# The seam between the second graph attention and the three mean layers of a graph network: loads issued in the attention's tail, weights folded on GpSimd, rows joined tile by tile

## The reference, cut to what matters

```
q, k, v = x @ Wq + bq, x @ Wk + bk, x @ Wv + bv
logits = sum(q[dst] * k[src], -1) / sqrt(256)
attn = segment_softmax(logits, dst)
agg = segment_sum(attn[:, None] * v[src], dst)
h = relu(agg + x @ Ws + bs)
deg = maximum(segment_sum(1, dst), 1)
prev, al, bn_scale = h, sigmoid(alpha_res), 1 / sqrt(1 + 1e-5)
for i in range(3):
    mean_nb = segment_sum(h[src], dst) / deg
    z = (mean_nb @ Wl[i] + bl[i] + h @ Wr[i]) * bn_scale * gamma[i] + beta[i]
    h = relu(al * z + (1 - al) * prev);  prev = h
```

## Time and profile before

| | us |
|---|---|
| median of three runs | 5805.68 (5805.16 to 5807.68) |
| profiled execution: first to last instruction (span) | 5815.3 |
| busy in it: PE 4527.7, DVE 3139.1, POOL 3070.9, ACT 1771.1 | |
| attention, first gather issued to last sum added | 1746.7 to 2311.8 |
| seam, last sum added to first transpose of the mean layers | 2311.8 to 2363.4 |

### The profile page before, as it was taken

How to read it: one execution, slowest core, us unless ns; L and a number is a source line. 1 busy time by engine, 2 the same in 40 slices (tenths; PEclk the granted TensorE clock), 3 DMA queues, 4 the chain that set the end, 5 groups by cost and what they waited for, 6 DMA issues and landing times. The chain is left out here.

```text
span 5815.3 us, 84987 instructions
## 1 busy us (share of the span) xinstructions
PE 4527.7 (78%) x23597; PEld 3556.5 (61%) x23598; DVE 3139.1 (54%) x8260; ACT 1771.1 (30%) x4407; POOL 3070.9 (53%) x2836
## 2 busy tenths in 40 slices
PE   3887568699987887799978789377377888688778
PEld 2777446577745665478667656255365777577655
DVE  5655567534246886422340289588625555455464
ACT  1000068233315776010013344276131222122221
POOL 1777777677747774000020267665314777577610
PEclk8555589799998999899978855599598999899988
DMA  3999756200027775468556656597264888688710
GB/s 105 329 331 320 236 168 208 53 1 1 1 80 226 236 235 180 137 192 264 180 192 186 171 174 213 184 339 261 93 201 134 261 267 262 191 259 266 243 30 28
DMA packets 663344, 1081.70 MB, mean 186 GB/s; under 512 B 98049, under 2 KB 453898, under 8 KB 662886
## 3 DMA queue, kind: packets, MB, share of 16 engines
q1 hardware_dynamic: 333574, 506.09, 28.3%
q0 software_dynamic: 135904, 356.79, 20.9%
q10 hardware_dynamic: 193536, 214.86, 10.3%
HBM read 767.10 MB, written 309.85 MB: 185 GB/s over the span
## 5 line engine op out<-in xcount | busy, mean ns | idle before, releaser
L2754 POOL DMA_INDIRECT max_rows<-tab,src_r x784 | 741.1, 945 | 312.6 <-issue 226.9
L403 POOL DMA_INDIRECT counts<-put_n,put_at x400 | 560.1, 1400 | 202.4 <-issue 134.8
L2796 PE MATMUL ps_t<-ident,max_rows 128*128 128x128 f32 x3136 | 434.0, 297 | 146.4 <-DMA max_rows<-tab,src_r 146.1
L2851 DVE TENSOR_TENSOR_SCAN run<-same,run,ps_t 128x256 f32<-128x256 bf16 x392 | 271.5, 734 | 468.1 <-PE ps_t L2796 468.1
L2796 PEld LDWEIGHTS ps_t<-ident,max_rows 128*128 128x128 f32 x3136 | 402.3, 208 | 174.3 <-DMA max_rows<-tab,src_r 173.6
L1317 POOL DMA_INDIRECT late_rows<-tab,src_a x416 | 420.3, 1010 | 146.1 <-issue 117.6
L707 POOL DMA_INDIRECT logit_rows<-tab,src_a x416 | 428.7, 1030 | 126.6 <-issue 115.0
L1054 POOL DMA_INDIRECT pair_rows<-tab_kv,src_a x416 | 401.3, 965 | 176.7 <-issue 117.3
L2247 POOL DMA_INDIRECT slot_rows<-xn,into x100 | 102.2, 1022 | 739.0 <-DVE into L2239 709.7
L1828 PE MATMUL ps_a<-side,blocks 128*128 128x512 f32 x1950 | 460.4, 392 | 0.8 <-PE ps_a L1828 0.6
L2831 ACT ACTIVATE back<-ps_b 128x512 f32<-128x512 f32 x392 | 212.8, 594 | 804.4 <-PE ps_b L2808 804.4
(11 more groups left out here) (519 smaller groups left out, 10226.8 us busy)
## 6 DMA issues: line engine op xcount, KB each, us to landing
blocks<-counts SPq DMA_DIRECT2D x390, 320.0 KB, 3.4
seg_rows<-back ACTq DMA_DIRECT2D x196, 512.0 KB, 5.1
slot_rows<-logit_rows ACTq DMA_DIRECT2D x104, 512.0 KB
edge_rows<-slot_rows SPq DMA_DIRECT2D x104, 512.0 KB
slot_rows<-late_rows SPq DMA_DIRECT2D x104, 512.0 KB
sum_rows<-slot_rows SPq DMA_DIRECT2D x104, 512.0 KB
counts<-zeros ACTq DMA_DIRECT2D x130, 320.0 KB
wf<-in_L_ffn_W SPq DMA_DIRECT2D x57, 512.0 KB
```

Of the source, the lines that this page charges most:

```text
L403: nc.gpsimd.indirect_dma_start(out=g.counts, out_offset=bass.IndirectOffsetOnAxis(ap=g.put_at[:, j:j + 1], axis=0), in_=g.put_n[:, j:j + 1 ...
L2754: nc.gpsimd.indirect_dma_start(out=rows[:, b * Q + j, :], out_offset=None, in_=table, in_offset=bass.IndirectOffsetOnAxis(ap=g.src_r[:, n ...
L2796: ins = t.matmul(ps_t[:, n % R, h, at:at + P], rows[:, b * Q + 2 * h + j, c * P:(c + 1) * P], g.ident[:], start=False, stop=c == KD - 1 an ...
L2851: v.tensor_tensor_scan(run[:, b, c, 0:HG], same[:, b, 0:HG], ps_t[:, n % R, 0, c * HG:(c + 1) * HG], run[:, (b - 1) % Q, c, GP - 1:GP], AL ...
```

## The change

- The loads of `bulk` move into `attend`. SP issues the one for `al` at the block's start, ahead of the 104 loads of `locs`. After the last product with q (`made` at 104) it issues the nine loads of gamma, beta, `bl` and the weights into the buffer of `q`, which nobody reads any more. After the last read of the gathered rows by DVE and by ACT (`read` and `copied` at 104) it issues the load of `tab_own` into the ring `pair_rows`, whose first 6400 of 8192 elements are now `h`. SP waits for that load before its part of the block ends.
- The sigmoid runs on ACT at the block's start. The folding runs on GpSimd behind the last gather.
- The call of `bulk` is gone, and with it two phase ends (its own, and that of the phase that held `q`).
- In `mean_layers` DVE inverts denominators and degrees, and joins h = h + acc * (1 / den) by tiles, three tiles ahead of the first evacuation and then one ahead of each of the next 22. ACT applies the relu by tiles (`enter`), and PE's turn(p) waits for it. The small buffers `new` and `new_t` lie in the rest of the ring.

```diff
-def attend(nc, g, table, q, acc, scale):
+def attend(nc, g, table, q, acc, scale, rows, seam):
...
-        rows = sb("pair_rows", [P, W, 2 * D], F32)
...
                         ).then_inc(got[b], 16)
+                seam.fold(pool)
 
             @block.sync
             def _(sp):
                 sp.dma_start(cut[:], g.cut_slots[0:SLOTS].rearrange("(c r l) -> r c l", r=CS, l=P)).then_inc(cut_in, 16)
+                seam.load_gate(sp)
                 for n in range(NG):
                     b = n % Q
                     if n >= Q:
                         sp.wait_ge(sel_set, n - Q + 1)
                     sp.dma_start(locs[:, b, :], g.loc_slots[n * GP:(n + 1) * GP].partition_broadcast(P)).then_inc(locs_in[b], 16)
+                sp.wait_ge(made, NG)
+                seam.load_weights(sp)
+                sp.wait_ge(read, NG)
+                sp.wait_ge(copied, NG)
+                seam.load_rows(sp)
 
             @block.scalar
             def _(act):
                 a = nc.scalar
+                seam.gate(act)
...
-def mean_layers(nc, g, h, hr, rdeg, w, rows):
+def mean_layers(nc, g, h, acc, rdeg, w, rows, spare):
...
-        new = sb("new", [P, 3, D], F32)
-        new_t = sb("new_t", [P, 2, KD, P], F32)
+        new = spare[:, 0:3 * D].rearrange("p (n d) -> p n d", n=3)
+        new_t = spare[:, 3 * D:3 * D + 4 * P].rearrange("p (n k c) -> p n k c", n=2, k=KD)
...
+        joined, entered = sem("joined"), sem("entered")
+        hr, den = acc[:, :, 0:D], acc[:, :, D]
...
                     if p >= NT:
                         pe.wait_ge(rectified, p - NT + 1)
+                    else:
+                        pe.wait_ge(entered, p + 1)
...
+                def enter(t):
+                    act.wait_ge(joined, t + 5)
+                    nc.scalar.activation(h[:, t, :], h[:, t, :], ACT.Relu).then_inc(entered, 1)
+
+                for t in range(3):
+                    enter(t)
                 for l in range(L):
                     for t in range(NT):
                         take(l * NT + t)
+                        if l == 0 and t + 3 < NT:
+                            enter(t + 3)
                     for t in range(NT if l < L - 1 else 0):
...
+                def join(t):
+                    v.scalar_tensor_tensor(h[:, t, :], acc[:, t, 0:D], den[:, t:t + 1], h[:, t, :], ALU.mult, ALU.add).then_inc(joined, 1)
+
+                v.tensor_scalar(den, den, 1e-20, None, ALU.max).then_inc(joined, 1)
+                v.tensor_scalar(rdeg[:], g.deg[:], 1.0, None, ALU.max).then_inc(joined, 1)
+                dve.wait_ge(joined, 2)
+                v.reciprocal(den, den).then_inc(joined, 1)
+                v.reciprocal(rdeg[:], rdeg[:]).then_inc(joined, 1)
+                dve.wait_ge(joined, 4)
+                for t in range(3):
+                    join(t)
                 dve.wait_ge(based, 1)
                 v.tensor_scalar(behind[:], behind[:], g.head[:], None, ALU.add).then_inc(based, 1)
                 dve.wait_ge(based, 2)
                 for l in range(L):
                     for t in range(NT):
+                        if l == 0 and t + 3 < NT:
+                            join(t + 3)
                         evacuate(l * NT + t)
...
+class Seam:
+    def __init__(self, nc, ph, g, q, h):
+        sb, sem = ph.sb, ph.sem
+        self.nc, self.g, self.h = nc, g, h
+        self.al, self.eye = sb("al", [P, 2], F32), sb("eye", [P, P], F32)
+        flat = q[:].rearrange("p t d -> p (t d)")
+        self.wlr = flat[:, 0:12 * D].rearrange("p (l k c) -> p l k c", l=3, k=KD)
+        self.gam, self.bet, self.bl = (flat[:, n * D:(n + 3) * D].rearrange("p (l d) -> p l d", l=3) for n in (12, 15, 18))
+        self.gate_in, self.gated, self.weights_in, self.h_in, self.folded = (
+            sem(x) for x in ("gate_in", "gated", "weights_in", "h_in", "folded"))
+    def load_gate(self, sp):
+        sp.dma_start(self.al[:, 0:1], row_bc(self.g.ins["L1_gnn_alpha_res"])).then_inc(self.gate_in, 16)
+    def gate(self, act):
+        act.wait_ge(self.gate_in, 16)
+        self.nc.scalar.activation(self.al[:, 0:1], self.al[:, 0:1], ACT.Sigmoid).then_inc(self.gated, 1)
+    def load_weights(self, sp):
+        ins = self.g.ins
+        sp.dma_start(self.gam, ins["L1_gnn_gamma"].rearrange("(l d) -> l d", l=3).partition_broadcast(P)).then_inc(self.weights_in, 16)
+        sp.dma_start(self.bet, ins["L1_gnn_beta"].rearrange("(l d) -> l d", l=3).partition_broadcast(P)).then_inc(self.weights_in, 16)
+        sp.dma_start(self.bl, ins["L1_gnn_bl"].partition_broadcast(P)).then_inc(self.weights_in, 16)
+        for l in range(3):
+            sp.dma_start(self.wlr[:, l, :, 0:D], by_partition(ins["L1_gnn_Wl"][l])).then_inc(self.weights_in, 16)
+            sp.dma_start(self.wlr[:, l, :, D:2 * D], by_partition(ins["L1_gnn_Wr"][l])).then_inc(self.weights_in, 16)
+    def load_rows(self, sp):
+        sp.dma_start(self.h, tile_rows(self.g.tab_own)).then_inc(self.h_in, 16)
+        sp.wait_ge(self.h_in, 16)
+    def fold(self, pool):
+        o, v = Order(pool, self.folded), self.nc.gpsimd
+        al, eye, gam, bet, bl, wlr = self.al, self.eye, self.gam, self.bet, self.bl, self.wlr
+        pool.wait_ge(self.gated, 1)
+        o.link(v.tensor_scalar(al[:, 1:2], al[:, 0:1], -1.0, 1.0, ALU.mult, ALU.add))
+        o.then(v.tensor_scalar(eye[:], self.g.ident[:], al[:, 1:2], None, ALU.mult))
+        pool.wait_ge(self.weights_in, 16 * 9)
+        o.then(v.tensor_scalar(gam, gam, float(1.0 / np.sqrt(1.0 + 1e-5)), None, ALU.mult))
+        o.link(v.tensor_scalar(bet, bet, al[:, 0:1], None, ALU.mult))
+        o.link(v.tensor_scalar(gam, gam, al[:, 0:1], None, ALU.mult))
+        o.then(v.tensor_tensor(bl, bl, gam, ALU.mult))
+        sides = wlr.rearrange("p l k (s d) -> p l (k s) d", s=2)
+        for l in range(3):
+            o.then(v.tensor_tensor(sides[:, l, :, :], sides[:, l, :, :], gam[:, l, :].unsqueeze(1).broadcast_to([P, 2 * KD, D]), ALU.mult))
+        o.wait()
+        o.then(v.tensor_tensor(bl, bl, bet, ALU.add))
+        for k in range(KD):
+            at = wlr[:, :, k, D + k * P:D + (k + 1) * P]
+            o.then(v.tensor_tensor(at, at, eye[:].unsqueeze(1).broadcast_to([P, 3, P]), ALU.add))
+        o.wait()
...
-        with Phase(nc) as p2:
-            q = p2.sb("q", [P, NT, D], F32)
...
-            attend(nc, g, g.tab_kv, q, acc, D ** -0.5)
-        h = sb("h", [P, NT, D], F32)
-        wlr = sb("wlr", [P, 3, KD, 2 * D], F32)
-        eye = sb("eye", [P, P], F32)
-        bl = sb("bl", [P, 3, D], F32)
         rdeg = sb("rdeg", [P, NT], F32)
-        al = sb("al", [P, 2], F32)
-        gam, bet = sb("gam", [P, 3, D], F32), sb("bet", [P, 3, D], F32)
...
-        mean_layers(nc, g, h, acc[:, :, 0:D], rdeg, wlr, bl)
+        q = sb("q", [P, NT, D], F32)
...
+        rows = sb("pair_rows", [P, W, 2 * D], F32)
+        h = rows[:].rearrange("p w d -> p (w d)")[:, 0:NT * D].rearrange("p (t d) -> p t d", t=NT)
+        seam = Seam(nc, ph, g, q, h)
+        attend(nc, g, g.tab_kv, q, acc, D ** -0.5, rows, seam)
+        mean_layers(nc, g, h, acc, rdeg, seam.wlr, seam.bl, rows[:].rearrange("p w d -> p (w d)")[:, NT * D:])
```

More of the change, by code:

```diff
@@ L2618, in gnn1 @@
-        h = sb("h", [P, NT, D], F32)
-        wlr = sb("wlr", [P, 3, KD, 2 * D], F32)
-        eye = sb("eye", [P, P], F32)
-        bl = sb("bl", [P, 3, D], F32)
-        rdeg = sb("rdeg", [P, NT], F32)
-        al = sb("al", [P, 2], F32)
-        gam, bet = sb("gam", [P, 3, D], F32), sb("bet", [P, 3, D], F32)
-        feat, den = acc[:, :, 0:D], acc[:, :, D]
-        across = lambda a: a.unsqueeze(2).broadcast_to([P, NT, D])
-        sides = wlr[:].rearrange("p l k (s d) -> p l (k s) d", s=2)
@@ L2628, in gnn1 @@
[L2628 to L2642, removed]
-             [("v", lambda v, l=l: v.tensor_tensor(sides[:, l, :, :], sides[:, l, :, :],
-                                                   gam[:, l, :].unsqueeze(1).broadcast_to([P, 2 * KD, D]), ALU.mult)) for l in range(3)] +
-             [("v", lambda v, at=at: v.tensor_tensor(at, at, eye[:].unsqueeze(1).broadcast_to([P, 3, P]), ALU.add))
-              for at in (wlr[:, :, k, D + k * P:D + (k + 1) * P] for k in range(KD))],
-             loads=[(h[:], tile_rows(g.tab_own)), (al[:, 0:1], row_bc(g.ins["L1_gnn_alpha_res"])), (gam[:].rearrange("p l d -> p (l d)"), row_bc(g.ins["L1_gnn_gamma"])),
-                    (bet[:].rearrange("p l d -> p (l d)"), row_bc(g.ins["L1_gnn_beta"]))] +
-             [(bl[:, l, :], row_bc(g.ins["L1_gnn_bl"][l])) for l in range(3)] +
-             [(wlr[:, l, :, 0:D], by_partition(g.ins["L1_gnn_Wl"][l])) for l in range(3)] +
-             [(wlr[:, l, :, D:2 * D], by_partition(g.ins["L1_gnn_Wr"][l])) for l in range(3)])
@@ L2652, in gnn1 @@
-        mean_layers(nc, g, h, acc[:, :, 0:D], rdeg, wlr, bl)
+        rdeg = sb("rdeg", [P, NT], F32)
+        q = sb("q", [P, NT, D], F32)
+        with Phase(nc) as p3:
+            k, own = p3.sb("k", [P, NT, D], F32), p3.sb("own", [P, NT, D], F32)
```

(4 more changed lines are left out.)

## The result

The changed kernel takes 5772.45 us (median of five, 5769.92 to 5774.76) against 5806.06 (5805.16 to 5807.68) for the kernel before: ratio 0.9949, 95% interval 0.9938 to 0.996. That is 33.6 us less, where 48.0 were forecast; the time lies outside the forecast range, which ended at 5766.

The account below looks back on a forecast made before the run. Bound: a chain of stages sharing nothing across a block's end, with a 51.6 us seam. First transpose 48.3 us earlier, less 0.3, gives 48.0; 5805.68 less that is 5757.7 us, range 5756 to 5760, 8 in 10 5752 to 5766.

Parts of the forecast that it names:

- The gain's sum: Seam and pass start: first transpose 48.3 us earlier, less 0.3 up to the first `project`, 48.0 us gained.
- What is left between the stages: Between attention and mean layers: one block end and one phase end, 1.2 us, bounds 0.7 and 1.6.
- The fold on GpSimd: In the attention's tail: 14.5 us, from 2295 to 2309.5, 2.3 us ahead of the last sum, costed at nothing.
- rival 2: In the attention's tail: the fold or its loads are late, 2.7 us lost (5760.4), up to 5764.7; chance 0.17.
- The factor between GpSimd and DVE: Price of moving the fold's work: 1.57 for a product of 1024 elements, 1.914 us on GpSimd against 1.220.
- The loads: In the attention's tail: weights landed by 2295, `h` at about 2304, 8 us ahead of 2311.8, costing nothing.
- The first transposes: Start of the mean layers: first transpose 2.1 us after the block's start, then 1.9 us to the first `project`.
- The joins in the pass: First pass over the tiles: DVE 1.7 us, ACT 0.8, joins three tiles ahead, so tiles stay 1.94 us apart.
- The head of the attention: Start of attention on ACT: wait for `al`, table load of 1.28 us and sigmoid stay under cover, costed at nothing.
- Rival 1: At the seam: PE's clock stays at 2.4 GHz instead of falling, 2.5 us more gained, 5755.2; chance 0.22.
- Rivals 3 and 4: Clock does not rise in first pass, 5800.4 (0.04 with other small gains); GpSimd many times dearer, 5820.9 at 80 us (0.02).

Follow-up runs that it names:

- the vectors first: Changed kernel plus a GpSimd drain ahead of the fold, joins five tiles ahead, and a separate semaphore for gamma, beta and `bl`: 5757.07 us; on another chip 5754.41.

## Why the prediction was wrong

By its own steps:

- **The gain's sum.** Forecast 48.0. The two losses of the seam and the one of the pass are 8.54 (drain) + 2.25 (fold behind the last sum) + 6.1 (pass) = 16.9 us, which leaves 31.1; the traces give 31.15, the medians 33.6. The rest of 2.5 us lies in stages ahead of the seam and behind it, and these stages vary by more between traces (3390.8 to 3399.9 us behind the pass).
- **What is left between the stages: wrong, the largest term.** I priced the block's end from the pairs before and after `bulk` (1.64 and 0.73 us). In both GpSimd had been idle for long when the block ended; in the first its drain had ended at 2282.9. Here GpSimd came to the block's end as the last engine, and its drain of 8.54 us was still to be made. I had written that in the tail GpSimd and the DMA queues "have nothing to do": from 2284.0 on that was so, but only because the drain had run before. The trace of before showed it in a view that I did not take, the one by the line of the block's end. The step that fails is the one that costs the fold by its length alone. Moved behind the gathers it also moved the drain, from 29 us of cover to none.
- **The fold on GpSimd: mis-sized.** 19.2 us, where I had 14.5 and 17.4 as the upper bound. The products of 1024 took 2.35 us, not 1.914: the 6400-element row, which would have given 2.19, was the nearer one. In the row that I took one operand is stretched over neighbouring elements; that this made it cheap is a guess that no run here tests. The three scalar steps took 6.5 us for my 3.5; I bounded them from above by a two-operand step, and they are dearer than one. The weights were complete 12.2 us after the first issue, for my 11. In the trace after, the fold thus ended 2.25 us late. This was rival 2 in kind and nearly in size (2.7).
- **The factor between GpSimd and DVE.** The trace after has 2.35 us for the product of 1024 elements that took DVE 1.225 in the trace of before (L2643): a factor of 1.92, where I had 1.57. The Trainium skill (GPSIMD Engine Reference, section 3.1) has two-operand steps 1.96 times slower on GpSimd; that was nearer to this case than my row. The Trainium skill (GPSIMD Engine Reference, section 4.1) says of steps with one input that "1-input is roughly line-rate"; here they took 2.2 us for the 768 elements that took DVE 0.62, 3.5 times as long, and the measurement decides.
- **The loads: right.** `h` landed at 2295.7, 8.0 us ahead of the last sum, as forecast; the weights landed some 1.2 us later than forecast, which is counted with the fold.
- **The first transposes: right.** 2317.72 - 2315.50 = 2.2 us from the block's start (2.1), and 1.71 to the first product (1.9).
- **The joins in the pass: wrong.** The work per engine was right, 1.7 us on DVE and 0.8 on ACT in 1.94. "The joins are three tiles ahead" was not: in DVE's order join t + 3 stands behind the evacuation of t - 1, and in ACT's order the copy of t + 1 stands behind relu t + 3. Counted in tiles between the product that starts the chain and the product that ends it, the lead is two, and the chain is longer than two products.
- **The head of the attention: right.** ACT was through with the sigmoid at 1745.2 and made its first copy at 1750.4; the gathers kept their pace.
- **Rival 1, the clock: the forecast held.** The clock was at half from 2305 until about 2322.

```profile
2321.00:2322.00 1.00, 1.00 (x3) 0.34 (x2) 0.00 (x0) 0.00 (x0) 0.00 (x0) 0.50 1.02 392
2322.00:2323.00 1.00, 1.00 (x5) 0.60 (x4) 0.32 (x1) 0.00 (x0) 0.00 (x0) 0.95 1.02 382
```

The granted clock is the third number from the end: 0.50 is 1.2 GHz and 1.00 is 2.4. It rose 4.4 us after the first transpose. With the longer seam PE stood still for 15 us, so this trace does not test whether 4.6 us alone would have let it fall. The two traces with the vectors first come near it: PE stood still for 4.4 us in both, and the clock, full until then, fell in both. In the first trace it fell within the microsecond of the first transpose (2306.18), in the one on the other chip just ahead of it (2304.14):

```profile
2306.00:2307.00 1.00, 0.82 (x4) 0.49 (x4) 1.00 (x4) 1.00 (x4) 0.00 (x0) 0.69 1.04 394
```

```profile
2303.00:2304.00 1.00, 0.00 (x0) 0.00 (x0) 0.96 (x4) 0.33 (x1) 0.00 (x0) 0.90 0.86 259
```

So in the two runs that had the short seam rival 1 did not come either.

Rivals 3 and 4 did not come.

## What to carry to other kernels

When work is put at the end of a block, ask what the engine still does there: read the sequencer rows of the block's last line in the trace before, since a drain that is hidden under another engine's tail is in no list of waits and is paid in full when the engine becomes the last. When two in-order engines hand work to each other in a pipelined loop, work per engine and tile does not say whether it keeps pace; write the chain from one product to the product that needs it, with what stands ahead of each member in its engine's order, and divide by the tiles between them. The drain's row and the order of the instructions were there before anything ran, so both losses could have been suspected. Both were mended by a small edit: one drain ahead of the fold and joins two tiles earlier gave 15 us.

## What the runs showed of the hardware

- GpSimd's drain at the end of the block with 416 gathers cost 8.5 us: it ended 8.6 us after the last gather where it followed the gathers at once, took 8.54 us where it came 37 us later behind other work, and took 0.05 us where one had been made before. In the changed kernel it did not wait for data, since the gathered rows had long been read.
- Without that drain the three next ones of GpSimd took 0.09, 0.04 and 0.25 us, and nothing else became longer; the gathers and the fold were waited for by semaphores there.
- In the trace of before the same can be read at other blocks, as the time from the last gather's end to the drain's: 8.6 us after 416 gathers from another table, 7.7 and 7.4 after 392, 3.3 after 240, 4.15 to 5.25 after four blocks of 50, 2.3 after 4. The longest came after the most gathers, but there was no fixed price for each. What sets the 8.5 us stays open.
- On GpSimd an in-place step with a scalar took 2.5 to 2.6 ns an element and a two-tensor product 2.1 to 2.3.
